# The boundary between two state-space batches and the head of the attention block, rearranged in a macaron block on one Trainium2 core

## The chip, the cores and the metric

The program runs on one NeuronCore of a Trainium2 chip. A core has a matrix engine (TensorE, PE in the profile), a vector engine (VectorE, DVE), a scalar engine (ScalarE, ACT), a general one (GpSimd, POOL) and a sync engine (SyncE, SP) that issues most of the DMA transfers. Each engine works through its own queue in order; engines meet at semaphores. The metric is the device time of one execution in microseconds. A profiled execution gives the time of every instruction, its "span" being the time from the first instruction to the last.

## What is computed

Two layers of a macaron network on x of 2 batches x 512 tokens x 256 features, each sublayer behind a layer norm:

```
x = x + 0.5 * ffn(norm(x))        # FFN0: silu(x W1) * (x W3), Hadamard transform, W2
x = x + state_space(norm(x))      # MAMBA
x = x + 0.5 * ffn(norm(x))        # FFN1
x = x + 0.5 * experts(norm(x))    # MOE0: 8 experts, top 2, and a shared one
x = x + attention(norm(x))        # ATTN: 16 heads, causal, ALiBi
x = x + 0.5 * experts(norm(x))    # MOE1
```

The state-space sublayer, cut to what matters (512 inner features, 16 states, 128 ranks):

```
xp, z = split(x @ W_in.T)
xc = silu(causal_conv4(xp) + conv_b)
dt, Bm, Cm = split(xc @ W_x.T)                 # 128, 16, 16 columns
delta = softplus(dt @ W_dt.T + b_dt)
h_t = exp(delta_t * A) * h_(t-1) + delta_t * B_t * xc_t     # over 512 tokens
y = (sum over states of h * C) + xc * Dp
out = (y * silu(z)) @ W_out.T
```

## The kernel before, in words

Every engine has its own program, written out by hand, and all waits are `wait_ge` on semaphores at constants. The stages run in the order FFN0(batch 0), MAMBA(0), MAMBA(1), FFN1(1), MOE0(0), MOE0(1), ATTN(0), MOE1(0), ATTN(1), MOE1(1); FFN0 of batch 1 and FFN1 of batch 0 are cut into "side pieces" that TensorE does inside the state-space loops. Features lie on partitions, 512 tokens along the free axis; the 512 inner features are four chunks c = 0 to 3 of 128.

**One state-space batch** (`mamba(b)` in each engine's program). Ahead of the loop, TensorE projects the four chunks of xc: `step_input(k)` adds chunk k to dt, `row_input(k)` adds chunk k to the 32 rows of B and C (three copies, 96 rows). For batch 1 these run in the last two steps of batch 0's loop and at the head of batch 1. ScalarE copies dt out of its bank (`dtT`), TensorE makes four delta products (`step_output(c)`), and ScalarE takes a softplus of each (`softplus(c)`, semaphore `delta`). The B rows are split into three bf16 parts by turns: ScalarE's `part(0..2)`, VectorE's `left(0..1)`. ScalarE's copy `c_rows` (semaphore `crows`) is what SP writes to DRAM and reads back broadcast over the partitions, one row of C a step. VectorE's (or for chunks 2 and 3 GpSimd's) `delta_input` makes dx = delta * xc.

**The loop** has 32 steps: half 0 (t = 0 to 15) does chunks 0 and 1 with state n = t, half 1 chunks 2 and 3. In step t:
- ScalarE: two exponentials `decay` (line 1534), three buffers deep, so it can be up to three steps ahead of the scans.
- TensorE: `broadcast_b(t+1)` (line 934) puts row n of B on all partitions of bank 0, after `mul` of step t; then `add_state(t-2)` (line 882) adds h * C into two banks of sums; then whatever else is placed in the step.
- VectorE: `times_b(t)` (line 2056), two products of dx with bank 0; `scan(t)` (line 2064), two scans.
- GpSimd: h * C (line 2391), three buffers deep.

In batch 1's loop there is more: TensorE opens batch 0's output banks with the residual (`open_state_output`), adds the four chunks of batch 0's output (`mamba_output(0, c)`, line 843, in the steps of `OUTPUT_AT`), opens the sums (`open_sums`, line 941, step 1) and projects the four gates of batch 1 (`mamba_gate(1, c)`, in the steps of `GATE_AT`; ScalarE copies them out raw in those of `GATE_OUT`, each ahead of its next step's exponentials). ScalarE takes batch 0's last sums out in step 1 (`sums_out(1, 0)`) and moves the residual out in step 7; VectorE's step 6 begins with the norm statistics of that residual. The banks of delta chunks 2 and 3 in batch 1 are 1 and 6, the same as batch 0's output banks.

**The late head** (`late_head`). In MOE0(1), TensorE goes through 13 blocks p: up products of chunk p, then point 0, then the broadcast of the expert weights and the down chunk p-2, then point 1. At these points it does the head of ATTN(0): two norm transposes (line 510), six projections of keys, queries and values, two value transposes (line 711), all through bank 7, each after the evacuation of the one before. ScalarE evacuates and casts, VectorE subtracts, SP writes the parts to DRAM and reads them back into the stacks of the score products.

Of the kernel before, what the change touches and what calls it, by code (L numbers as in the profile page):

```python
# [59 lines left out]
GATE_AT, GATE_OUT = (1, 4, 6, 8), (4, 7, 9, 11)  # L60
NORM_BANKS = ((7, 1), (1, 6))
OUTPUT_AT = (0, 1, 2, 3)
# [13 lines left out]
LATE_NORM_AT, LATE_HEAD_AT, EARLY_CAST_AT = 3, 5, 4  # L76
START_PRODUCTS, TAIL_PRODUCTS = 4, (8, 12)
EPS = 1e-5
HEAD = 4
# [74 lines left out]
def build(nc, x, W_in, conv_w, conv_b, W_x, W_dt, b_dt, A_log, Dp, W_out, W1, W2, W3, Wq, bq, Wk, bk,  # L154
          Wv, bv, Wo, bo, gate_w, w1, w2, w3, sw1, sw2, sw3, const_f, const_b, aux_q, aux_k, out):
    ctx = ExitStack()
    with ctx:
# [279 lines left out]
        class TensorProgram:  # L437
# [277 lines left out]
            def late_head(self, p, point):  # L715

                pe = self.pe
                if p == LATE_NORM_AT + 1:
                    pe.wait_ge(S[MOE0]["prod"], HEAD + MM + SECOND_MIXED + 1)
                    self.norm_transpose(2 * ATTN + 1, point)  # L720
                if LATE_HEAD_AT <= p < LATE_HEAD_AT + 3:
                    i = 2 * (p - LATE_HEAD_AT) + point
                    self.head_projection(0, i, LATE_BANKS[i], i)
                if p == LATE_HEAD_AT + 3:
                    self.head_values(0, point, 7, 6)
# [132 lines left out]
            def mamba(self, b):  # L858
# [60 lines left out]
                else:  # L919
                    step_input(3).then_inc(s["dt"], 1)  # L920
                    row_input(3).then_inc(s["bc"], 1)
# [31 lines left out]
                else:  # L953
                    add_state(STEPS - 1, 0)
                    pe.wait_ge(s["delta"], 2 * EC)
                for t in range(STEPS):
# [13 lines left out]
                    if b == 1:  # L970
                        if t in OUTPUT_AT:
                            if t == OUTPUT_AT[0]:
                                self.open_state_output(0)
                            self.mamba_output(0, OUTPUT_AT.index(t))
# [11 lines left out]
                    if b == 0 and t == STEPS - 2:  # L986
                        step_input(0, 1)
                        step_input(1, 1)
                    if b == 0 and t == STEPS - 1:
                        step_input(2, 1)  # L990
                        for k in range(EC - 1):
                            row_input(k, 1)
# [180 lines left out]
        class ScalarProgram:  # L1173
# [189 lines left out]
            def late_head(self, p):  # L1363

                if p == LATE_NORM_AT + 1:
                    self.norm_evacuate(2 * ATTN + 1, 0)
                first = LATE_HEAD_AT
                if first <= p < first + 3:
                    for i in (2 * (p - first), 2 * (p - first) + 1):
                        self.head_evacuate(0, i, LATE_BANKS[i])  # L1370
                if p == first + 3:
                    for c in range(DC):
                        self.head_values(0, c, 7)
# [86 lines left out]
            def mamba(self, b):  # L1460
# [28 lines left out]
                else:  # L1489
# [4 lines left out]
                    self.mamba_silu(1, 3)  # L1494
                act.wait_ge(s["dt"], b + 1)
# [1122 lines left out]
```

## Time and profile before

| | us |
|---|---|
| three timed runs | 796.66, 796.93, 798.0 |
| their median | 796.93 |
| the profiled execution's own time | 796.57 |
| its span | 794.8 |
| TensorE, VectorE, ScalarE, GpSimd busy in it | 708.7, 548.7, 405.4, 243.1 |

Times in the profile are counted from the start of its span. PE is TensorE's matmuls, PEld its weight loads, which overlap them. Matmul records overlap, so the time that a matmul takes of the engine is read from start to start. An fp32 matmul shows as two records. "idle before <-releaser" names what ended the engine's wait. "PEclk" is the clock granted to TensorE as a share of 2.4 GHz.

### The profile page before, as it was taken

The page shows a single profiled execution, that of the slowest core. Times are in us where ns is not written, and L with a number is a line of the kernel's source. Part 1 is how long each engine was busy: PE and PEld are TensorE (multiplying, and loading weights), DVE is VectorE, ACT ScalarE, POOL GpSimd, SP SyncE. Part 2 cuts the span into 40 slices and gives each one's busy share as a digit, 9 for nine tenths or more (in the row PEclk, how much of TensorE's full clock was granted, in tenths as well). Part 3 has the DMA queues.
Part 4 walks back from the last instruction along what each step waited for, and adds up shares of the span by engine and source line. Part 5 has one row for each costly group of instructions (what it writes and reads, how often), then busy time and mean ns, then how long its engine had stood idle before and what let it go on. Part 6 is the DMA issues. An engine that isn't in the chain of part 4 may idle for free.

```text
span 794.8 us, 10884 instructions
## 1 busy us (share of the span) xinstructions
PE 708.7 (89%) x4044; PEld 485.9 (61%) x4067; DVE 548.7 (69%) x962; ACT 405.4 (51%) x594; POOL 243.1 (31%) x190
## 2 busy tenths in 40 slices
PE   3899998796789699989999998997889999788998
PEld 3587664451325255547877887885447887434787
DVE  4544489999969999985448566367855656954644
ACT  3454597777447787751233344351476442274322
POOL 0001148777527677970799000001000001000000
PEclk9999999996899899999999999998999999899999
DMA  8300022223102222216100100043000033000000
GB/s 285 137 2 0 1 57 79 79 69 76 56 22 73 67 71 76 79 55 201 46 1 1 23 1 1 14 111 104 15 1 1 15 95 115 18 28 1 1 1 26
DMA packets 30609, 41.78 MB, mean 53 GB/s; under 512 B 3769, under 2 KB 19971, under 8 KB 30531
## 3 DMA queue, kind: packets, MB, share of 16 engines
q1 hardware_dynamic: 29306, 40.91, 16.9%
q8 instruction: 32, 0.52, 0.3%
q10 hardware_dynamic: 1252, 0.19, 0.2%
q14 instruction: 19, 0.16, 0.1%
HBM read 36.73 MB, written 4.26 MB: 52 GB/s over the span
## 4 chain that ended last, share of the span: by engine, by line
PE 54%; DVE 15%; issue 15%; ACT 7%; DMA 4%; POOL 2%; SPq 1%; another core or an unknown queue 0%; DVEq 0%; POOLq 0%; ACTq 0%
PE PS L500 32%; DVE PS L2056 4%; PE PS L605 3%; DVE shared L2064 3%; PE PS L1088 3%; PE PS L1071 2%; DVE route L2114 2%; POOL shared L2391 2%; DMA shared<-scratch_q 2%; PE PS L649 2%; ACT shared L1608 2%; PE PS L458 1%; PE PS L882 1%; DMA route<-scratch_c 1%; DMA shared<-in_L_ffn_W_dram 1%
## 5 line engine op out<-in xcount | busy, mean ns | idle before, releaser
L2391 POOL TENSOR_TENSOR shared<-shared,route 128x1024 f32<-128x1024 f32 x64 | 150.7, 2358 | 71.1 <-DVE shared L2064 71.1
L2064 DVE TENSOR_TENSOR_SCAN shared<-shared,PS 128x512 f32<-128x512 f32 x128 | 148.7, 1203 | 2.4 <-ACT shared L1534 1.7
L500 PE MATMUL PS<-xnT,work_r 128*128 128x512 f32 (+1 forms) x596 | 149.9, 398 | 0.3
L500 PE MATMUL PS<-xnT,weights_r 128*128 128x256 f32 (+1 forms) x732 | 148.6, 351 | 1.4 <-issue 1.1
L500 PEld LDWEIGHTS PS<-xnT,weights_r 128*128 128x128 f32 x732 | 114.4, 193 | 47.7 <-issue 33.4
L500 PEld LDWEIGHTS PS<-xnT,work_r 128*128 128x128 f32 (+1 forms) x596 | 109.2, 188 | 24.9 <-DVE gated L1788 1.6
L1534 ACT ACTIVATE shared<-shared,cols 128x512 f32<-128x512 f32 x128 | 85.0, 714 | 25.9 <-DVE shared L2064 25.4
L500 PE MATMUL PS<-weights_r,work_r 128*128 128x256 f32 (+1 forms) x624 | 88.6, 293 | 0.3 <-DVE work_r L1795 0.3
L2056 DVE TENSOR_TENSOR PS<-shared,PS 128x512 f32<-128x512 f32 x128 | 81.3, 681 | 3.4 <-PE PS L934 3.0
L500 PEld LDWEIGHTS PS<-weights_r,work_r 128*128 128x128 f32 (+1 forms) x624 | 80.4, 190 | 2.2 <-issue 0.6
L882 PE MATMUL PS<-shared,cf 64*64 64x512 f32 x512 | 75.9, 665 | 0.6 <-POOL shared L2391 0.6
L2477 POOL MEMSET shared<- 128x512 f32 x2 | 1.1, 526 | 222.8 <-DMA scratch_q<-shared 117.6
L1788 DVE TENSOR_TENSOR gated<-gated,PS 128x512 f32<-128x512 f32 (+1 forms) x48 | 32.8, 684 | 36.0 <-ACT gated L1253 35.9
L934 PE MATMUL PS<-combT,cb 96*128 96x512 bf16 x64 | 26.0, 407 | 34.1 <-DVE PS L2056 33.2
L1260 ACT ACTIVATE work_r<-gated 128x512 fp32r<-128x512 f32 (+1 forms) x48 | 30.3, 631 | 50.5 <-DVE gated L1913 41.2
L1253 ACT ACTIVATE gated<-PS 128x512 f32<-128x512 f32 (+1 forms) x48 | 28.5, 594 | 47.2 <-PE PS L500 47.0
L2114 DVE TENSOR_REDUCE route<-PS 128x2 f32<-128x256 f32 (+2 forms) x64 | 48.1, 819 | 2.2 <-PE PS L1052 1.2
L1795 DVE TENSOR_TENSOR work_r<-gated,work_r 128x512 fp32r<-128x512 f32 (+1 forms) x48 | 34.3, 716 | 20.8 <-ACT work_r L1260 20.2
L934 PEld LDWEIGHTS PS<-combT,cb 96*128 96x128 bf16 x64 | 6.3, 98 | 55.5 <-DVE PS L2056 50.6
L1913 DVE TENSOR_TENSOR gated<-gated,PS 128x512 f32<-128x512 f32 x40 | 27.4, 686 | 16.0 <-remote 14.6
L1803 DVE TENSOR_TENSOR shared<-gated,PS 128x512 f32<-128x512 f32 x16 | 10.9, 687 | 39.0 <-PE PS L605 34.7
L1608 ACT ACTIVATE shared<-PS 128x1280 f32<-128x1280 f32 x20 | 24.8, 1238 | 20.5 <-PE PS L1075 18.4
(224 smaller groups left out, 1049.9 us busy)
## 6 DMA issues: line engine op xcount, KB each, us to landing
route<-scratch_c SPq DMA_DIRECT2D x64, 256.0 KB, 3.2
shared<-in_L_ffn_W_dram SPq DMA_DIRECT2D x3, 1024.0 KB, 8.9
scratch_k<-shared SPq DMA_DIRECT2D x12, 128.0 KB
scratch_q<-shared SPq DMA_DIRECT2D x12, 128.0 KB
shared<-scratch_k SPq DMA_DIRECT2D x8, 192.0 KB
shared<-scratch_q SPq DMA_DIRECT2D x8, 192.0 KB
mamba_w<-in_L_ffn_w_dram SPq DMA_DIRECT2D x2, 704.0 KB, 5.3
beside<-in_L_ffn_w_dram SPq DMA_DIRECT2D x2, 704.0 KB, 7.8
```

Source lines behind the costliest of these rows:

```text
L500: last = nc.tensor.matmul(o, lhs[l], rhs[r], start=(start and i == 0), stop=(stop and i == 2))
L882: last = nc.tensor.matmul(bank(SUM_BANKS[j])[o, :], ident[r, r], hc[r, (t % H_SLOTS * 2 + j) * T:(t % H_SLOTS * 2 + j + 1) * T], start=Fal ...
L934: nc.tensor.matmul(bank(B_BANK), pick[0:96, n:n + 1].broadcast_to([96, P]), bc_stack[0:96, :], start=True, stop=True).then_inc(s["B"], 1)
L1260: nc.scalar.activation(ring[p % RING][0][0:rows, :], gated[0:rows, slot * T:(slot + 1) * T], ACT.Copy)\
L1534: nc.scalar.activation(decay[t % D_SLOTS][:, j * T:(j + 1) * T], delta_of[b][c], ACT.Exp, scale=c_A[:, n + c * DS:n + c * DS + 1]).then_in ...
L1608: nc.scalar.activation(pT[h % P_SLOTS], bank(score_bank(h), 3)[:, 0:PT_COLS], ACT.Exp)\
L1788: return nc.vector.tensor_tensor(g, g, bank(2 + slot if rows == P else slot)[0:rows, :], ALU.mult)
L1795: nc.vector.tensor_tensor(lo[0:rows, :], gated[0:rows, slot * T:(slot + 1) * T], hi[0:rows, :], ALU.subtract).then_inc(s["hid"], 1)
L2056: v.tensor_tensor(products[:, j * T:(j + 1) * T], dx[:, c * T:(c + 1) * T], bank(B_BANK), ALU.mult).then_inc(s["mul"], 1)
L2064: v.tensor_tensor_scan(hst[:, (t % 2 * 2 + j) * T:(t % 2 * 2 + j + 1) * T], decay[t % D_SLOTS][:, j * T:(j + 1) * T], products[:, j * T:(j ...
L2114: v.reduce_max(m_all.rearrange("p (h c) -> p h c", c=TC)[:, bass.ds(g * 2, 2), qc], tile, AX.X).then_inc(s["max"], 1)
L2391: nc.gpsimd.tensor_tensor(hc[:, u * 2 * T:(u * 2 + n) * T].rearrange("p (c t) -> p c t", c=n), hst[:, (t % 2) * 2 * T:(t % 2 * 2 + n) * T] ...
```

## The change

Five edits, each on the engines that it concerns:
1. Batch 1's row products: in step 30, two low-rank and two row products (before: two low-rank); in step 31 the other two of each (before: one low-rank, three row products; the last of each at the head of batch 1).
2. ScalarE loads the Softplus table ahead of the wait for dt, not behind the dt copy; a wait for batch 0's third-last state sum is added there; softplus(1) goes ahead of the C rows' copy.
3. In batch 1, softplus(2) and softplus(3) move into the loop behind step 2's exponentials, between a load of the Softplus table and one of the table with exp. The waits for them change: TensorE waits for two softplus ahead of the loop and for all four in step 2; VectorE no longer waits for the third ahead of step 0.
4. Batch 0's outputs go to steps 2, 2, 3, 3 (before 0, 1, 2, 3), the opening of their banks to step 2 (before 0); batch 1's gates to steps 3, 5, 6, 8 (before 1, 4, 6, 8), copied out in 6, 7, 9, 11 (before 4, 7, 9, 11).
5. The late head's pieces start at point 1 of block 4 and take one point each. Before, both transposes took block 4, the projections blocks 5 to 7, the value transposes block 8.

```diff
-GATE_AT, GATE_OUT = (1, 4, 6, 8), (4, 7, 9, 11)
+GATE_AT, GATE_OUT = (3, 5, 6, 8), (6, 7, 9, 11)
-OUTPUT_AT = (0, 1, 2, 3)
+OUTPUT_AT, LATE_DELTA = (2, 2, 3, 3), 2
-LATE_NORM_AT, LATE_HEAD_AT, EARLY_CAST_AT = 3, 5, 4
+LATE_NORM_AT, LATE_SLOT, LATE_HEAD_AT, EARLY_CAST_AT = 3, 9, 5, 4
...
             def late_head(self, p, point):        # TensorE
                 pe = self.pe
-                if p == LATE_NORM_AT + 1:
+                i = 2 * p + point - LATE_SLOT
+                if i == 0:
                     pe.wait_ge(S[MOE0]["prod"], HEAD + MM + SECOND_MIXED + 1)
-                    self.norm_transpose(2 * ATTN + 1, point)
-                if LATE_HEAD_AT <= p < LATE_HEAD_AT + 3:
-                    i = 2 * (p - LATE_HEAD_AT) + point
-                    self.head_projection(0, i, LATE_BANKS[i], i)
-                if p == LATE_HEAD_AT + 3:
-                    self.head_values(0, point, 7, 6)
+                if 0 <= i < DC:
+                    self.norm_transpose(2 * ATTN + 1, i)
+                if DC <= i < DC + 6:
+                    self.head_projection(0, i - DC, LATE_BANKS[i - DC], i - DC)
+                if DC + 6 <= i < 2 * DC + 6:
+                    self.head_values(0, i - DC - 6, 7, 6)
...
                 else:                             # TensorE, batch 1
-                    step_input(3).then_inc(s["dt"], 1)
-                    row_input(3).then_inc(s["bc"], 1)
                     pe.wait_ge(s["dtT"], 2)
...
                     add_state(STEPS - 1, 0)
-                    pe.wait_ge(s["delta"], 2 * EC)
+                    pe.wait_ge(s["delta"], EC + 2)
...
-                        if t in OUTPUT_AT:
-                            if t == OUTPUT_AT[0]:
-                                self.open_state_output(0)
-                            self.mamba_output(0, OUTPUT_AT.index(t))
+                        if t == OUTPUT_AT[0]:
+                            pe.wait_ge(s["delta"], 2 * EC)
+                            self.open_state_output(0)
+                        for c in range(EC):
+                            if OUTPUT_AT[c] == t:
+                                self.mamba_output(0, c)
...
                     if b == 0 and t == STEPS - 2:
                         step_input(0, 1)
                         step_input(1, 1)
+                        row_input(0, 1)
+                        row_input(1, 1)
                     if b == 0 and t == STEPS - 1:
                         step_input(2, 1)
-                        for k in range(EC - 1):
-                            row_input(k, 1)
+                        row_input(2, 1)
+                        step_input(3, 1).then_inc(s["dt"], 1)
+                        row_input(3, 1).then_inc(s["bc"], 1)
...
             def late_head(self, p):               # ScalarE
-                if p == LATE_NORM_AT + 1:
-                    self.norm_evacuate(2 * ATTN + 1, 0)
                 first = LATE_HEAD_AT
-                if first <= p < first + 3:
-                    for i in (2 * (p - first), 2 * (p - first) + 1):
-                        self.head_evacuate(0, i, LATE_BANKS[i])
-                if p == first + 3:
-                    for c in range(DC):
-                        self.head_values(0, c, 7)
+                for i in (2 * p - LATE_SLOT, 2 * p + 1 - LATE_SLOT):
+                    if 0 <= i < DC:
+                        self.norm_evacuate(2 * ATTN + 1, 0, (i,))
+                    if DC <= i < DC + 6:
+                        self.head_evacuate(0, i - DC, LATE_BANKS[i - DC])
+                    if DC + 6 <= i < 2 * DC + 6:
+                        self.head_values(0, i - DC - 6, 7)
...
+                nc.scalar.preload_act_table(ACT.Softplus)          # ScalarE, mamba(b)
                 act.wait_ge(s["dt"], b + 1)
+                act.wait_ge(s["ys"], HEAD + b * (STEPS - 2))
                 nc.scalar.activation(dtT, bank(DT_BANK[b]), ACT.Copy).then_inc(s["dtT"], 1)
-                nc.scalar.preload_act_table(ACT.Softplus)
...
                 part(1, 64, bc_rest)
+                softplus(1)
                 nc.scalar.activation(c_rows, bank(BC_BANK[b])[0:2 * DS, :], ACT.Copy).then_inc(s["crows"], 1)
-                softplus(1)
                 act.wait_ge(s["left"], 2 * b + 2)
                 part(2, 32, bc_rest)
-                softplus(2)
-                softplus(3)
+                if b == 0:
+                    softplus(2)
+                    softplus(3)
...
+                    if b == 1 and t == LATE_DELTA:
+                        nc.scalar.preload_act_table(ACT.Softplus)
+                        softplus(2)
+                        softplus(3)
+                        nc.scalar.preload_act_table_set("natural_log_exp_and_others")
...
                 first_input(1)                    # VectorE, mamba(b)
-                dve.wait_ge(s["delta"], b * EC + 3)
+                if b == 0:
+                    dve.wait_ge(s["delta"], 3)
```

## Rows read from the trace of the kernel before

**Rows 1.** The page: busy time of each engine, and the chain of waits by engine.
```profile
PE 708.7 (89%) x4044; PEld 485.9 (61%) x4067; DVE 548.7 (69%) x962; ACT 405.4 (51%) x594; POOL 243.1 (31%) x190
...
PE 54%; DVE 15%; issue 15%; ACT 7%; DMA 4%; POOL 2%; SPq 1%; another core or an unknown queue 0%; DVEq 0%; POOLq 0%; ACTq 0%
```

**Rows 2.** Windows: us; busy time (instructions) of PE, PEld, DVE, ACT, POOL; clock; DMA.
```profile
237.80:354.30 116.50, 102.12 (x595) 56.51 (x591) 114.50 (x145) 86.56 (x124) 89.08 (x45) 0.96 0.24 73
...
470.90:542.00 71.10, 68.42 (x378) 56.86 (x382) 38.90 (x85) 34.36 (x57) 0.53 (x1) 1.00 0.16 43
```

**Rows 3.** Waits of VectorE, both state-space batches: us in total, times, longest.
```profile
DVE shared L2033 <- ACT combT L1510: 5.3, 1, 5.3
```

**Rows 4.** Timeline of VectorE, head of batch 1: start, us, what [idle before].
```profile
237.81 1.29 DVE L2056 TENSOR_TENSOR PS<-shared,PS 128x512 f32<-128x512 f32 x2 [1.38 <-PE PS L934]
239.49 2.33 DVE L2064 TENSOR_TENSOR_SCAN shared<-shared,PS 128x512 f32<-128x512 f32 x2 [0.38 <-ACT shared L1534]
...
246.67 2.33 DVE L2064 TENSOR_TENSOR_SCAN shared<-shared,PS 128x512 f32<-128x512 f32 x2 [0.24 <-POOL shared L2391]
...
252.33 1.27 DVE L2056 TENSOR_TENSOR PS<-shared,PS 128x512 f32<-128x512 f32 x2
...
255.75 1.27 DVE L2056 TENSOR_TENSOR PS<-shared,PS 128x512 f32<-128x512 f32 x2
```

**Rows 5.** Windows, the end of batch 0's loop.
```profile
222.40:231.30 8.90, 8.90 (x28) 3.21 (x24) 5.54 (x7) 1.22 (x2) 4.70 (x2) 0.91 0.00 0
```

**Rows 6.** Timeline of ScalarE at the boundary.
```profile
230.71 0.60 ACT L1496 ACTIVATE shared<-PS 128x512 f32<-128x512 f32 x1 [5.47 <-PE PS L864]
231.33 1.28 ACT L1497 ACT_TABLE_LOAD   x1
232.62 0.59 ACT L1510 ACTIVATE combT<-PS 96x512 bf16<-96x512 f32 x1
...
234.57 0.57 ACT L1517 ACTIVATE shared<-PS 32x512 f32<-32x512 f32 x1
...
236.14 1.23 ACT L1506 ACTIVATE shared<-PS,cols 128x512 f32<-128x512 f32 x2
...
238.68 2.56 ACT L1534 ACTIVATE shared<-shared,cols 128x512 f32<-128x512 f32 x4
```

**Rows 7.** Timeline of TensorE at the boundary.
```profile
235.28 1.10 PE L889 MATMUL PS<-shared 128*128 128x512 f32 x2 [1.08 <-ACT shared L1517]
...
237.33 0.39 PE L934 MATMUL PS<-combT,cb 96*128 96x512 bf16 x1
```

**Rows 8.** Timeline of TensorE, steps 1 and 2 of batch 1.
```profile
243.29 1.88 PE L941 MATMUL PS<-shared,skips 128*128 128x512 f32 x4
245.01 1.89 PE L843 MATMUL PS<-shared 128*128 128x256 f32 x8
...
248.12 0.39 PE L934 MATMUL PS<-combT,cb 96*128 96x512 bf16 x1
248.44 1.09 PE L882 MATMUL PS<-shared,cf 64*64 64x512 f32 x8
249.46 1.99 PE L843 MATMUL PS<-shared 128*128 128x256 f32 x8
```

**Rows 9.** Windows, steps 5 to 8 of batch 1 (granted clock behind POOL).
```profile
258.70:261.56 2.86, 0.00 (x0) 0.00 (x0) 2.78 (x12) 2.20 (x3) 2.86 (x2) 1.00 0.26 92
261.60:268.40 6.80, 5.22 (x16) 2.27 (x16) 6.80 (x11) 4.42 (x8) 2.60 (x2) 0.50 0.12 41
```

**Rows 10.** Timeline of TensorE, block 4 of MOE0(1).
```profile
490.76 0.63 PE L510 MATMUL PS<-cf,xn_tok 128*128 128x128 f32 x4 [1.69 <-issue]
...
493.76 0.63 PE L510 MATMUL PS<-cf,xn_tok 128*128 128x128 f32 x4 [0.74 <-DVE xnT L1771]
```

**Rows 11.** Timeline of VectorE in the same block.
```profile
489.27 1.38 DVE L1759 TENSOR_SCALAR xn_tok<-x_tok,stats 128x256 f32<-128x256 f32 x4
...
492.93 0.68 DVE L1771 TENSOR_TENSOR xnT<-PS,xnT 128x512 fp32r<-128x512 f32 x1
```

## The prediction, made before the changed kernel was run

> **What bounds the kernel now.** I read the page first: TensorE is busy 89% of the span and leads the chain of waits, with VectorE second [rows 1]. A share over the span says little about one boundary, so next came the windows by stage. In the second state-space batch (237.80 to 354.30) VectorE is busy 114.50 of 116.50 us, TensorE 102.12; in the second batch of the first expert stage (470.90 to 542.00) TensorE is busy 68.42 of 71.10 us, VectorE 38.90 [rows 2]. So the two places that the diff touches have different limits: there a microsecond counts if VectorE gets it, here if TensorE does. The table of VectorE's waits over both state-space batches is led by one single wait of 5.3 us, for ScalarE's first part copy at the head of the second batch [rows 3]: that is the boundary. The timelines of the boundary, engine by engine, give the sizes.
>
> VectorE's clock in the loop is one step: two products with B (line 2056), two scans (line 2064), 3.42 us from 252.33 to 255.75. Step 0 of the second batch starts at 237.81, step 5 at 255.75; I call these starts T0 and T5 [rows 4]. The loop has one hard coupling: broadcast_b(t+1) stands at the head of TensorE's step t and its one bank is free only when step t's products are done. Whatever TensorE does after broadcast_b(t+1) must be over before broadcast_b(t+2), or step t+2 starts late.
>
> **Row products in the last two steps: nothing.** Eight products and one add_state lie between 222.4 and 231.3, and TensorE is busy 8.90 of these 8.90 us [rows 5]. The change reorders them; the dt row is still the last but one, so ScalarE's copy of dt stays at about 230.71. The two low-rank row products now wait for the third silu, done before 225. The new wait on ys asks for an add_state that precedes dt in the same queue: nothing.
>
> **ScalarE across the boundary: a gain of 0.4 at T0, 1.3 by T2.** The Softplus table load (1.28 us at 231.33, after the dt copy) moves into the idle 5.47 us before that copy [rows 6]. The first part copy then starts when the bc row is ready, about 231.57 instead of 232.62. From there I follow the chain with the old durations and hand-overs: softplus(0) 232.53, the first remainder 232.27 to 232.95, part 1 at 233.1, softplus(1) 233.64, the C rows, now behind softplus(1), 234.21 to 234.78 (before, 234.57 to 235.14), part 2 ends at 235.3. TensorE's step_output(3) waits for the C rows: 0.36 earlier than 235.28. Add_state and broadcast_b(0) follow 2.05 later, so T0 moves from 237.81 to 237.45 [rows 4, 6, 7]. Two softplus (1.23 us) leave the path ahead of the exponentials: these start near 236.6 instead of 238.68, which removes the scan's 0.38 us wait; the sums, the GpSimd gate products behind them and GpSimd's step 0 come 2 us earlier, which removes a 0.24 us wait at step 2 [rows 6]. T1 = 240.87 and T2 = 244.29; step 2's scan comes near 245.4 instead of 246.67, 1.3 earlier.
>
> The same swap at the first batch is worth nothing: there the bc row comes later than the load, and step 0 waits for work that stays in place.
>
> **The two late softplus inside the loop: nothing.** ScalarE ends the sums at 241.0, step 2 at 242.2, then a load, two softplus (done at 244.75), a load (245.95), step 3's exponentials to 247.2. The scan that needs them starts near 248.9, and TensorE's new wait is reached after 246.9. If that cover were gone, the cost would be the 3.8 us of the insert.
> The Trainium skill (ScalarE: Activation LUTs, What ACT_TABLE_LOAD costs) adds a drain of about 1.4 us to every switch. In this trace the copy follows its load without it (231.33 + 1.28, next at 232.62). By the page the insert would end 2.8 us later, at the edge of that scan.
>
> **Four output products in two steps instead of four: the loss.** TensorE's matmuls overlap in the records, so I count from start to start [rows 8]: broadcast 0.32, add_state 1.02, a two-bank opening 1.72 (243.29 to 245.01), the next output and gate group together 3.11 (245.01 to 248.12), of which I give the output 1.71 and the gate 1.40; before a broadcast 0.1 more. The old order had open + output in step 0, opening + output + gate in step 1 (4.8), one output each in 2 and 3. The new one is empty in step 0, 2.0 in step 1, and then:
> step 2: 0.32 + 1.02 + 1.72 + 2 x 1.71 + 0.1 = 6.6 us;
> step 3: 0.32 + 1.02 + 2 x 1.71 + 1.40 + 0.1 = 6.3 us.
> VectorE takes 3.42 for each. Broadcast_b(3) can't go before step 2's products are through, T2 + 1.32 = 245.6. So broadcast_b(5) goes at 245.6 + 12.9 = 258.5, and T5, 0.45 later, is 258.9. Old T5: 255.75. That is **+3.2 us** with all of it at full clock, the 1.3 of gain already inside. What waits behind: every later broadcast, add_state and side product on TensorE, hence VectorE's steps 4 and 5. After step 3 only one gate lies in a step, so nothing more is lost, and nothing is won back: VectorE is the limit for the remaining 26 steps. ScalarE stands at raw gate 0 until about 259, then delivers the residual about 1 us before VectorE's statistics want it.
>
> **The clock: 0 to 1.5 us more.** The granted clock was 1.00 while TensorE idled from 258.70 to 261.56, and then 0.50 (1.2 instead of 2.4 GHz) from 261.60 to 268.40 [rows 9]. The new steps 0 and 1 leave TensorE idle from about 239.3 to 242.2. If the low level falls on the opening, broadcast and add_state behind that gap, these 3 us of work take up to twice as long, of which up to 1.5 us reaches T5. I laid low stretches of half and of all the length of that row over the new steps at ten positions, each beginning within 4 us after 240: they give 0.1 to 1.65 more, mean 0.8. I take 0.9.
> The Trainium skill (TensorE: Matmul & The Clock Gate, HAM oscillation — how this bites in real kernels) says that waits between bursts make the next burst start cold; the trace agrees (0.50 after 2.9 us of nothing). It speaks against bunching these products.
>
> **The late head half a block on: -2.4 us.** In block 4 TensorE finished the up products at 489.07, stood 1.69 us before the first norm transpose, did it, the broadcast and the down chunk in 2.26 (493.76 less 0.74 less 490.76), and stood 0.74 before the second transpose [rows 10]. The transposes wait for VectorE's scaled rows (489.27 + 1.38 = 490.65) and low halves (492.93 + 0.68 = 493.61) [rows 11]. Half a block on, broadcast and down chunk (2.26 less 0.4 for the transpose) fill the first wait, the transpose follows at about 490.9, the next up products, some 2.9 us, fill the second, until 494. Both waits go: 2.43. The second transpose at 494, ScalarE's evacuation and VectorE's low half put the first projection's input at about 496.1, and TensorE is there at about 496: 0.1 back. Projections and value transposes are the same count at the same price; their evacuations and casts come about 2.5 us earlier too, so the writes and stack loads on SP's queue shift with them. The bounds: 0 if each wait reappears, 2.5 if none does. I take 2.4, since TensorE has no other wait until 542.
>
> **Sum against the profiled execution** (796.57 us, span 794.8): +3.2 + 0.9 - 2.4 = +1.7. The median of the runs is 796.93, 0.36 above the profiled one, so 798.6. This kernel's runs can tell about 0.2%, 1.6 us, from no change; the forecast stands on that edge.
>
> **Rivals.**
> 1. Forecast: overfull steps with a partly slow clock, both head waits gone. +1.2 to +2.4, 798.1 to 799.3. Chance 0.45.
> 2. The same, but the clock stays at 2.4 GHz: +3.2 - 2.4 = +0.8, 797.7. For it: the low stretch may fall into the gap itself. Against: gaps of 2.9 us did lower it. 0.20.
> 3. The head's waits only move: the first projection waits for ScalarE's late evacuation in block 5. +3.2 + 0.7 = +3.9, 800.8. Against: the order worked out above leaves 0.1. 0.12.
> 4. More waits in steps 5 to 9: ScalarE, held at raw gate 0, is late with the residual, so VectorE's statistics wait, or a low clock falls on the side products: +1 on the forecast, 799.6. The margin is about 1 us. 0.11.
> 5. Faster: VectorE keeps its 1.3 and the bunched outputs are absorbed, -1.3 - 2.4 = -3.7, 793.2. This needs steps 2 and 3 on TensorE at no more than about 4 us each; above that T5 slips. Against: 3.11 us for one output and one gate. For: the old step 1 took 4.8 and VectorE didn't stop. 0.06.
> 6. The parts cancel or are hidden elsewhere, 796.9. 0.06.
>
> **From these:** slower by over 0.2%: 0.25 of case 1, 3 and 4, together 0.48; within: 0.20 of case 1, 2 and 6, together 0.46; faster: 0.06. Range 796.8 to 800.8: cases 1, 2, 4, 6 and half of 3.
>
> **What would show it.** T0 near 237.45, T2 near 244.3; then VectorE waiting twice for the broadcast, about 2.5 and 2.5 us, T5 at 259 to 260.4; a clock of 0.50 somewhere in 240 to 248; exponentials without waits; in block 4 of the expert stage no wait before either transpose. I am wrong if VectorE's steps 3 to 5 stay 3.42 apart, or if TensorE waits anew at the first projection.

## The result, and the profile after

The changed kernel is slower. Over 11 runs of each the median went from 797.03 to 801.18 us, 4.15 apart (the means are 3.5 apart). The ratio on record is 1.0038 with a 95% interval of 1.0024 to 1.0052, which is 1.9 to 4.1 us, 3.0 in the middle; the text goes by this ratio. I had forecast +1.7 (798.6), a range of 796.8 to 800.8, and a chance of 0.48 for slower. From the forecast's base of 796.93 the ratio leads to 800.0, inside the range; the median of the 11 runs lies 0.4 above its top. The profiled execution, 802.7 us with a span of 800.9, is the slowest of its 11 runs, while that of before, 796.57, lies a little under its median. So the 6.1 us between the two traces are more than the 3.0 between the kernels, and part of the work below was to find which of the 6.1 belong to the change.

I followed VectorE's instructions through both traces, each against the same instruction of before, and noted by how much it starts later:

| place | before | after | shift |
|---|---|---|---|
| T0, step 0 of batch 1 | 237.81 | 236.91 | -0.9 |
| T4 | 252.33 | 253.34 | +1.0 |
| T5 | 255.75 | 259.62 | +3.9 |
| step 20 | 311.98 | 318.41 | +6.4 |
| MOE0(0), up to its fifth block | 411 to 440 | | +6.1 to +8.2 |
| MOE0(1), ahead of the late head | 487 | | +8.6 |
| MOE0(1), behind it | 529.34 | | +6.0 |
| end of the span | | | +6.1 |

The view that shows the first step is VectorE's timeline after [rows 4]; each line is start, duration, what, and in brackets the wait ahead of it.

```profile
236.91 1.29 DVE L2067 TENSOR_TENSOR PS<-shared,PS 128x512 f32<-128x512 f32 x2 [2.26 <-PE PS L933]
...
253.34 1.29 DVE L2067 TENSOR_TENSOR PS<-shared,PS 128x512 f32<-128x512 f32 x2 [2.65 <-PE PS L933]
...
259.62 1.29 DVE L2067 TENSOR_TENSOR PS<-shared,PS 128x512 f32<-128x512 f32 x2 [2.76 <-PE PS L933]
```

The two waits of 2.65 and 2.76 us for broadcast_b (line 933 now) are the two that the forecast put there at about 2.5. TensorE's timeline says why [rows 8]:

```profile
238.35 0.38 PE L933 MATMUL PS<-combT,cb 96*128 96x512 bf16 x1 [0.46 <-DVE PS L2067]
241.68 0.61 PE L933 MATMUL PS<-combT,cb 96*128 96x512 bf16 x1 [2.95 <-DVE PS L2067]
242.08 3.62 PE L940 MATMUL PS<-shared,skips 128*128 128x512 f32 x4
245.49 0.63 PE L933 MATMUL PS<-combT,cb 96*128 96x512 bf16 x1
246.06 1.66 PE L883 MATMUL PS<-shared,cf 64*64 64x512 f32 x8
247.64 1.98 PE L856 MATMUL PS<-x_tok,cf 128*128 128x512 f32 x4
249.47 3.62 PE L844 MATMUL PS<-shared 128*128 128x256 f32 x16
252.92 0.38 PE L933 MATMUL PS<-combT,cb 96*128 96x512 bf16 x1
253.23 1.09 PE L883 MATMUL PS<-shared,cf 64*64 64x512 f32 x8
254.25 3.72 PE L844 MATMUL PS<-shared 128*128 128x256 f32 x16
257.62 1.74 PE L500 MATMUL PS<-xnT,weights_r 128*128 128x512 f32 x6
259.20 0.39 PE L933 MATMUL PS<-combT,cb 96*128 96x512 bf16 x1
```

From broadcast to broadcast, step 2 takes 7.43 us (245.49 to 252.92) and step 3 6.28 (252.92 to 259.20). Forecast were 6.6 and 6.3 at full clock. The difference in step 2 is the clock: the broadcast at 245.49 takes 0.63 instead of 0.38, add_state 1.66 instead of 1.09. It was low from the gap in step 1 on [rows 9]; windows of us, busy time (instructions) of PE, PEld, DVE, ACT, POOL, granted clock, DMA:

```profile
238.95:242.00 3.05, 0.32 (x1) 0.33 (x2) 3.05 (x5) 2.97 (x6) 2.76 (x3) 0.74 0.07 28
242.00:247.30 5.30, 5.30 (x14) 1.45 (x13) 5.30 (x7) 5.26 (x7) 4.34 (x2) 0.50 0.22 49
```

ScalarE did what it should: the loads and the two softplus of step 2 are done at 245.6, and its wait at raw gate 0 ends at 259.39 [rows 6].

```profile
241.76 1.28 ACT L1565 ACT_TABLE_LOAD   x1
243.05 1.26 ACT L1510 ACTIVATE shared<-PS,cols 128x512 f32<-128x512 f32 x2
244.33 1.28 ACT L1568 ACT_TABLE_LOAD   x1
245.63 3.78 ACT L1539 ACTIVATE shared<-shared,cols 128x512 f32<-128x512 f32 x6
...
259.39 0.60 ACT L1506 ACTIVATE shared<-PS 128x512 f32<-128x512 f32 x1 [7.95 <-PE PS L500]
...
261.11 1.07 ACT L1574 ACTIVATE x_tok<-PS 128x512 f32<-128x512 f32 x2
```

The residual is out at 262.2 and VectorE's statistics begin at 263.08 without a wait. The late head has lost both waits [rows 10]; TensorE's timeline, in which a down chunk (12 records of 256 columns), the first transpose (line 510), the up products (512 columns) and the second transpose follow one another:

```profile
497.56 1.78 PE L500 MATMUL PS<-weights_r,work_r 128*128 128x256 f32 x12
499.31 0.63 PE L510 MATMUL PS<-cf,xn_tok 128*128 128x128 f32 x4
499.70 3.03 PE L500 MATMUL PS<-xnT,work_r 128*128 128x512 f32 x12
502.56 0.60 PE L510 MATMUL PS<-cf,xn_tok 128*128 128x128 f32 x4
```

What I had not forecast is the jump at step 20. Long behind the change, TensorE opens the sums of the second half (line 940) in its step 18, behind broadcast_b(19), and that opening waits for ScalarE to empty the banks. First the trace of before, TensorE and VectorE:

```profile
307.09 1.98 PE L941 MATMUL PS<-shared,skips 128*128 128x512 f32 x4 [1.18 <-ACT shared L1542]
...
311.55 0.39 PE L934 MATMUL PS<-combT,cb 96*128 96x512 bf16 x1
```

```profile
311.98 1.29 DVE L2056 TENSOR_TENSOR PS<-shared,PS 128x512 f32<-128x512 f32 x2 [0.86 <-PE PS L934]
```

Then the changed kernel, in the same order:

```profile
309.59 0.39 PE L933 MATMUL PS<-combT,cb 96*128 96x512 bf16 x1
311.88 3.59 PE L940 MATMUL PS<-shared,skips 128*128 128x512 f32 x4 [1.90 <-ACT shared L1547]
...
316.45 1.69 PE L500 MATMUL PS<-xnT,weights_r 128*128 128x256 f32 x12
317.98 0.39 PE L933 MATMUL PS<-combT,cb 96*128 96x512 bf16 x1
```

```profile
318.41 1.29 DVE L2067 TENSOR_TENSOR PS<-shared,PS 128x512 f32<-128x512 f32 x2 [3.23 <-PE PS L933]
```

The opening took 3.59 us and not 1.98, the side products (line 500) follow it, and broadcast_b(20) comes at 317.98; VectorE's step 20 waits 3.23 us for it. In the trace of before the same wait was 0.86 us, with an opening of 1.98 us behind a wait of 1.18.

### The profile page after: what moved, and what is told of

It reads as the page before. It is cut to its first block, busy times and chain, and to the rows that moved or that the text cites. A ratio compares the mean times of both kernels' runs of the same rounds, so it can differ in the third digit from the quotient of the medians.

```text
span 800.9 us, 10910 instructions
## 1 busy us (share of the span) xinstructions
PE 714.7 (89%) x4067; PEld 488.7 (61%) x4067; DVE 550.7 (69%) x962; ACT 408.0 (51%) x596; POOL 242.2 (30%) x190
## 4 chain that ended last, share of the span: by engine, by line
PE 65%; DVE 14%; issue 10%; ACT 7%; DMA 2%; POOL 1%; SPq 0%; DVEq 0%; POOLq 0%; ACTq 0%
PE PS L500 36%; DVE PS L2067 4%; PE PS L605 3%; PE PS L883 3%; DVE route L2125 3%; PE PS L1092 3%; PE PS L1075 2%; DVE shared L2075 2%; PE PS L649 2%; PE PS L844 2%; PE PS L865 2%; ACT shared L1618 2%; ACT shared L1539 1%; PE PS L767 1%; PE PS L458 1%
## 5 line engine op out<-in xcount | busy, mean ns | idle before, releaser
L1805 DVE TENSOR_TENSOR work_r<-gated,work_r 128x512 fp32r<-128x512 f32 (+1 forms) x48 | 36.5, 761 | 18.5 <-ACT work_r L1264 18.0
```

The costliest lines, as they stand in the source:

```text
L1805: nc.vector.tensor_tensor(lo[0:rows, :], gated[0:rows, slot * T:(slot + 1) * T], hi[0:rows, :], ALU.subtract).then_inc(s["hid"], 1)
```

## The experiments

All ratios are to the kernel before, timed on the same chip. "Shift" is again VectorE's, in the profiled execution, against the trace of before.

**The parts, one by one.** Five kernels, each with some of the five edits of the diff:

```diff
 e1: before + edit 5 (late head)
 e2: after - edit 5
 e3: before + edit 1 (row products) + edit 2 (table load, softplus(1))
 e4: before + edits 1, 2 and 5
 e5: before + edit 4:
-GATE_AT, GATE_OUT = (1, 4, 6, 8), (4, 7, 9, 11)
+GATE_AT, GATE_OUT = (3, 5, 6, 8), (6, 7, 9, 11)
-OUTPUT_AT = (0, 1, 2, 3)
+OUTPUT_AT = (2, 2, 3, 3)
```

> The kernel before with the late head alone half a block on. Theory A (each edit is worth what its own place shows, the head takes two waits of 1.69 and 0.74 us off TensorE in block 4): 2.4 us faster than before, no wait before either norm transpose, nothing changed up to 489. Theory B (the head's waits only move and the rest of the fall between 497 and 503 in the changed kernel is something else): within 0.5 us of before.

Measured: 0.9986, interval 0.9964 to 1.0009. The shift goes from +1.09 at 487 to -1.41 at 529: **-2.50 us across the head**. The same difference stands in every one of the ten traces with edit 5, -2.47 to -2.51, and it is 0.0 in those of e2, e3 and e5. The ratio alone could not have said so; the trace does.

> The changed kernel with the late head put back. Theory A: slower than before by the boundary alone, +4 at step 5 and with what a low clock adds behind it +4 to +7, so 2.4 slower than the changed kernel. Theory B: the same as the changed kernel, +3 to +4. If the wait at step 20 belongs to the boundary, it is here too.

Measured: 1.0054, interval 1.0029 to 1.0080. T0 -1.4, T5 +3.5, step 20 +6.15, and +6.3 from 487 to 536 without the head's gain. So the change's loss is in the state-space part, and the late head gives back part of it. The trace ends at +8.7: 1.8 of that comes between 536 and 600, most of it at the collision told of further down, which this execution had.

> The kernel before with the row products in the last two steps, the Softplus table ahead of the dt copy and softplus(1) ahead of the C rows; all four softplus, the outputs and the gates where they were. Theory A: step 0 starts 0.5 to 0.9 earlier, the scan's 0.38 wait goes, and the kernel is 0.8 to 1.3 us faster. Theory B (VectorE's earlier start is given back to TensorE at steps 1 to 3, which carries 4.8 us in step 1, or at the wait of step 19 or 20): within 0.4 us of before.

Measured: 0.9996, interval 0.9974 to 1.0017. T0 -0.9, and -0.9 to -1.2 from there to the attention block. What VectorE has at T0 is carried, but it is too small for the ratio, which excludes neither theory; and the last part shows that only 0.4 of it comes from the edits.

> The two together, without the late softplus and the bunched outputs. Theory A: the sum of the two, 3.2 to 3.7 us faster than before, about 793.5. Theory B: one of the two is given back, 1 to 2.4 us faster.

Measured: 0.9954, interval 0.9936 to 0.9972: faster than both kernels, as theory A had it. T0 -1.4, behind the head -4.0.

> The kernel before with the outputs in steps 2, 2, 3, 3, their banks opened in step 2 and the gates in steps 3, 5, 6, 8 (out in 6, 7, 9, 11), nothing else. Theory A (the bunched products are the whole loss): steps 0 to 3 start where they did, VectorE waits for the broadcast at steps 4 and 5, step 5 starts 3.7 to 4.7 later than before, and with the wait at step 20 the kernel is 4 to 6.5 us slower. Theory B (the loss comes from the two softplus and their table loads in ScalarE's step 2, or from both together): less than 2 us slower.

Measured: 1.0085, interval 1.0054 to 1.0115 over 7 runs. T0 +0.05, T4 +1.2, **T5 +4.1**, flat from there on to 354. The profiled execution was one of the two fastest of the seven (800.57 of 799.36 to 806.72), so its trace has less in it than the ratio, and no jump at step 20. The ratio is +4.3 to +9.2 us, which fits theory A and not B. The bunched outputs alone make the loss at T5; without edits 1 to 3 it is no smaller. Between T0 and T5 the clock was low only from 242.7 to 246.1 here, ahead of step 2's broadcast, and the two overfull steps take 6.61 us (246.53 to 253.14) and 6.29 (253.14 to 259.43).

**The clock in the gap.** In e6 TensorE does bf16 products into an idle bank in the empty steps 0 and 1; nobody reads them.

```diff
+                        if t < 2:
+                            self.idle_products(7, (10, 6)[t])
                         if t == OUTPUT_AT[0]:
```

> The changed kernel with products that nobody reads on TensorE in steps 0 and 1 of batch 1 (ten and six, 128x512 bf16, into the free bank 7, behind the broadcast of each step). They fill the idle stretch of 3 us ahead of the opening of the sums. Theory A: the granted clock stays at 1.00 between 237 and 248, the opening takes 1.7 instead of 3.4 us, step 5 starts about 1 us earlier (+2.9 instead of +3.9), and the kernel is 1 us faster than the changed one, more if the later low stretches go too. Theory B (the low stretch costs nothing there, since the two bunched steps wait for VectorE anyway): step 5 at the same time within 0.2.

Measured: 1.0023, interval 1.0003 to 1.0044. TensorE's timeline and two windows of e6:

```profile
239.25 2.32 PE L517 MATMUL PS<-cb 128*128 128x512 bf16 x10
...
242.59 1.88 PE L940 MATMUL PS<-shared,skips 128*128 128x512 f32 x4
...
245.78 0.39 PE L933 MATMUL PS<-combT,cb 96*128 96x512 bf16 x1
...
252.39 0.38 PE L933 MATMUL PS<-combT,cb 96*128 96x512 bf16 x1
...
258.68 0.39 PE L933 MATMUL PS<-combT,cb 96*128 96x512 bf16 x1
```

```profile
238.90:247.30 8.40, 7.46 (x32) 2.88 (x33) 8.40 (x10) 8.28 (x12) 7.12 (x4) 1.00 0.18 63
307.00:315.00 8.00, 6.42 (x38) 3.87 (x37) 7.60 (x9) 7.32 (x11) 6.01 (x4) 1.00 0.27 76
```

With the gap filled the clock stays at 2.4 GHz, the opening takes 1.88 us instead of 3.62, and the two overfull steps take 6.61 us (245.78 to 252.39) and 6.29 (252.39 to 258.68): the forecast's 6.6 and 6.3. From T0 to T5 VectorE needs 21.52 us, against 22.71 after and 17.94 before. So of the 4.8 us that the change adds between T0 and T5, 3.6 are the count of products in two steps and 1.2 the low clock. T5 itself came at +3.4 and not at the +2.9 expected, as T0 lay 0.7 later than in the trace of the change; and the ratios of e6 and the change overlap, so the 1.2 rests on the traces. At step 18 the clock is full too, and the shift does not grow there.

**Another spread of the same work.** The outputs over steps 2, 3, 4, 4, and the first gate pushed on to step 5.

```diff
-GATE_AT, GATE_OUT = (3, 5, 6, 8), (6, 7, 9, 11)
+GATE_AT, GATE_OUT = (5, 6, 7, 8), (6, 7, 9, 11)
-OUTPUT_AT, LATE_DELTA = (2, 2, 3, 3), 2
+OUTPUT_AT, LATE_DELTA = (2, 3, 4, 4), 2
```

> The changed kernel with outputs in steps 2, 3, 4, 4 and gates in 5, 6, 7, 8 (out in 6, 7, 9, 11); the two softplus stay in step 2. Theory A: TensorE's steps take 4.8, 3.1, 4.8, 2.9 us, VectorE's step 5 starts where it would without any wait (about 254.0, 5.6 earlier than in the changed kernel); the residual is then late for VectorE's statistics in step 6 by 1 to 2 us; in all 3.5 to 4.5 us faster than the changed kernel. Theory B (the inserted table loads are what holds the loop): no faster than the changed kernel by more than 1 us.

Measured: 1.0170, interval 1.0142 to 1.0198, by far the slowest: my expectation failed. T5 was at 256.66, only 0.9 late, as I had wanted, but then ScalarE and VectorE (timelines of e7):

```profile
263.88 0.60 ACT L1506 ACTIVATE shared<-PS 128x512 f32<-128x512 f32 x1 [10.74 <-PE PS L500]
...
265.60 1.07 ACT L1574 ACTIVATE x_tok<-PS 128x512 f32<-128x512 f32 x2
```

```profile
266.71 0.42 DVE L1722 BATCH_NORM_STATS2 stats<-x_tok 128x6 f32<-128x256 f32 x1 [6.55 <-issue]
...
279.13 0.18 DVE L1758 RECIPROCAL stats<-stats 128x4 f32<-128x4 f32 x1 [6.61 <-ACT stats L1229]
```

ScalarE stands at raw gate 0 for 10.74 us, because the gate is now one of TensorE's last products before it. The residual's copy is behind that gate in ScalarE's queue, and VectorE's step 6 begins with the statistics of that residual: 6.55 us of waiting, where I had expected 1 to 2. This is the mechanism of the forecast's rival 4. In the change itself it has a margin of 0.9 us (262.2 to 263.08); here it is overdrawn. The same happens once more: ScalarE waits 9.10 us for raw gate 1, the square root of the statistics (line 1229) stands behind it, and VectorE's reciprocal at 279.13 waits 6.61 us for that, with TensorE's clock at 0.50 from 265.8 to 276.0. These two waits are most of what VectorE loses from T5 (+0.9) to step 14 (+16.4), and the jump at step 20 adds 2.1.

**The queue at step 18.** In e8, which is the whole change otherwise, the side products of step 18 go ahead of the opening, where they fill TensorE's wait for ScalarE.

```diff
+                    if b == 1 and t == DS + 2:
+                        for n in pieces_at(b, t):
+                            self.side_piece(b, n)
                     if t == DS + 2:
                         pe.wait_ge(s["yr"], b * 4 + 2)
...
-                    for n in pieces_at(b, t):
+                    for n in pieces_at(b, t) if (b, t) != (1, DS + 2) else ():
```

> The changed kernel with the side products of batch 1's step 18 ahead of the opening of the second sums instead of behind it. Theory A (the second loss, 2.4 us at step 20, is a queue on TensorE: it stands idle for ScalarE's copies of the sums with work behind it, falls to the low clock and opens the sums at half speed): the idle 1.9 us shrinks below 0.6, the opening takes 1.7, step 20's wait of 3.2 goes, 2 to 3 us faster than the changed kernel. Theory B (VectorE waits for something else there): no difference beyond 0.5 us.

Measured: 0.9999, interval 0.9981 to 1.0017, where the change has 1.0038 and, in the repeat below, 1.0032. T5 +4.1, step 20 +3.5: the loss at step 20 is gone, and of the wait of 0.86 us that was there before, 0.11 is left. The interval lies clear of the change's first one and overlaps that of its repeat a little. TensorE's timeline of e8:

```profile
309.79 0.39 PE L933 MATMUL PS<-combT,cb 96*128 96x512 bf16 x1
309.83 1.77 PE L500 MATMUL PS<-xnT,weights_r 128*128 128x256 f32 x12
312.13 1.98 PE L940 MATMUL PS<-shared,skips 128*128 128x512 f32 x4 [0.52 <-ACT shared L1550]
...
315.06 0.39 PE L933 MATMUL PS<-combT,cb 96*128 96x512 bf16 x1
```

**The gains together, and two repeats.** e9 is e4 with the edit of step 18; e10 is e4 once more; e11 is the change once more. The expectation of e9 names the last two softplus inside the loop among its parts; the kernel that ran does not have them there (it has edits 1, 2 and 5, as e4).

> The kernel before with the edits to the row products, to ScalarE's order (the table load ahead of the dt copy, softplus(1) ahead of the C rows, the last two softplus inside the loop) and the late head, the outputs left at steps 0 to 3, and with batch 1's side products of step 18 placed ahead of the opening of the second half's sums. My theory: the parts add. The ScalarE and head edits alone gave 0.9954; in the kernel before, VectorE waited 0.86 us at step 20 for the broadcast behind the opening, and this wait goes, so about 0.9 us more: ratio 0.994 to the kernel before, VectorE's shift constant from step 5 to step 31. Rival: the opening no longer has a wait to fill, the side products only change places and the broadcast of step 20 is as late as before: ratio 0.9954 and the shift constant too, but the wait of 0.86 us still there.

> The kernel with the edits to the row products, ScalarE's order and the late head alone, once more, on the same chip as the kernel with the step 18 placement added, so that the two can be compared. Expected: ratio 0.9954 to the kernel before again, within 0.9936 to 0.9972; if the step 18 placement is worth 0.9 us, the other one lies 0.001 below this one; if it is worth nothing, they agree.

> The whole change once more, beside the others on one chip. My theory says +3.9 at step 5 (bunched outputs with a partly low clock), about +2.4 at step 20 where the opening of the second sums holds the broadcast while TensorE's clock is low, some +1.8 in the expert stage between, and -2.5 at the late head; ratio about 1.004. Rival to the part at step 20: it is a chance of that one execution. Then this profile shows no growth of VectorE's shift between steps 12 and 31, and the runs scatter over 3 us with or without it.

Measured: e9 0.9946, 0.9926 to 0.9966, median 793.17 and its 6 runs from 792.62 to 794.52. e10 0.9977, 0.9954 to 1.0000, median 795.65 and its 12 runs from 791.05 to 800.52. e11 1.0032, 1.0010 to 1.0054, 10 runs from 796.91 to 803.75. e10's ratio lies just above the 0.9936 to 0.9972 that I expected from e4, the same kernel. Their intervals overlap, and what the traces give to that kernel's edits, 0.4 us at the boundary and 2.5 at the head, is 0.9964, between the two. Two things follow from the traces. e11's has +5.05 from T0 to T5 (238.22 to 261.21) and +2.5 at step 20, so the loss at step 20 isn't a chance of one execution; of the +1.8 expected in the expert stage it has +0.8. And e10's trace, of a kernel **without** bunched outputs, shows the jump at step 20 too: the shift goes from -0.9 to +1.5 there, where in e4 it stays at -1.4. So the jump isn't the change's own. Windows of e10, then of e4, at the same two places:

```profile
276.60:283.40 6.80, 6.49 (x26) 3.50 (x30) 6.52 (x9) 3.01 (x5) 3.49 (x3) 0.51 0.25 58
307.20:310.60 3.40, 3.40 (x8) 0.87 (x11) 3.03 (x4) 3.38 (x5) 2.04 (x1) 0.50 0.29 97
```

```profile
277.70:281.10 3.40, 3.40 (x20) 2.61 (x12) 3.40 (x5) 1.44 (x2) 2.07 (x1) 0.50 0.23 77
304.50:309.40 4.90, 3.73 (x19) 1.68 (x19) 4.90 (x6) 4.84 (x7) 3.31 (x2) 1.00 0.16 58
```

In e10 the low stretch of steps 10 to 12 lasts 6.8 us, TensorE and ScalarE come out of it some 0.7 us further behind VectorE, the opening of step 18 waits 1.92 us instead of 1.17, and the clock falls as it begins: 3.58 us instead of 1.98. Of the eleven traces whose side products stand behind the opening and whose schedule is otherwise that of before from step 9 on, five (after, e2, e7, e10, e11) had the long stretch, a longer wait of 1.6 to 1.9 us and the slow opening, and six (before, e1, e3, e4, e5, e6) a low stretch of 3.4 us, 1.2 us of waiting and the fast one. What makes the stretch long or short stays open. With the side products ahead, the long stretch came as well in e8 and e9, 6.8 us, and cost nothing: the wait is 0.5 or 0.3 us and the opening takes 1.98. VectorE has no wait at step 20 in e9's trace, so the rival in that expectation is out. e9's six runs lie within 1.9 us, but e8's twelve, with the same edit, scatter over 5.0 (794.80 to 799.75), so it isn't shown that the edit narrows the runs; nor can its 0.86 us be told from the ratios of e9 and e10, whose intervals overlap.

**A collision that e9's trace showed.** At 536 the profiled execution of e9 lost 1.7 us to something new. VectorE and GpSimd, timelines of e9:

```profile
536.48 2.73 DVE L1954 TENSOR_TENSOR work_r<-gated,work_r 128x256 fp32r<-128x256 f32 x2 [0.27 <-ACT work_r L1286]
```

```profile
536.23 2.37 POOL L2488 TENSOR_TENSOR x_tok<-x_tok,bo_all 128x1024 f32<-128x1024 f32 x1
```

Two subtractions that take 0.76 us elsewhere took 2.73, and TensorE waited 1.50 us for them. GpSimd's add stands behind a wait for writes to DRAM, and starts between 536 and 558 us in these traces. In e12 it waits for VectorE:

```diff
                 pool.wait_ge(xn_done, 2 * ATTN + b + 1)
+                if b == 0:
+                    pool.wait_ge(S[MOE0]["hid"], HEAD + 2 * MM)
```

> The kernel before with the edits to the row products, to ScalarE's order ahead of the loop and to the late head, with batch 1's side products of step 18 ahead of the opening, and with one wait more: GpSimd adds the attention's output bias to batch 0's tokens only after VectorE's last low halves of the second expert batch. In the profile without that wait the add of 2.37 us began 0.25 us ahead of VectorE's two subtractions of 256 columns, these took 2.73 us instead of 0.76, and TensorE's last down products waited 1.50 us for them. My theory: the two engines share the way to SBUF in such operations, so with the wait the subtractions take 0.76 us again in every execution, TensorE has no wait there, and the executions in which the two met get 1.7 us faster: median 792.5 to 793.2 against about 797.3 for the kernel before, ratio 0.9935 to 0.9945. Rival: the slow subtractions had another cause, such as a DMA into the same tiles: then they are seen at 2.7 us again in some executions. Second rival: the later add now meets VectorE's residual or its attention work and costs the same there: no gain, and an operation of VectorE behind 537 longer than before.

Measured: 0.9948, interval 0.9928 to 0.9968, median 792.72 and 6 runs from 791.47 to 794.01. Timelines of VectorE and GpSimd in e12:

```profile
535.49 0.76 DVE L1954 TENSOR_TENSOR work_r<-gated,work_r 128x256 fp32r<-128x256 f32 x2 [0.28 <-ACT work_r L1286]
...
537.91 1.29 DVE L1784 SCALAR_TENSOR_TENSOR x_tok<-PS,x_tok 128x512 f32<-128x512 f32 x2 [1.67 <-PE PS L500]
```

```profile
537.94 2.35 POOL L2490 TENSOR_TENSOR x_tok<-x_tok,bo_all 128x1024 f32<-128x1024 f32 x1
```

The subtractions take 0.76 us, and the residual beside the add takes 1.29 as ever (one of its inputs is in PSUM). The ratio is that of e9, and just above the 0.9935 to 0.9945 expected: the collision was rare, in 2 of the 13 other traces (e2 and e9), so the median can't show it, and one trace of e12 isn't proof that it can't come back.

## Why the forecast came out as it did

The mechanism was right and its sizes nearly so; a loss further on was missing.

- **Row products, ScalarE across the boundary.** Forecast T0 237.45, measured 236.91 [rows 4, 6]. From the start of the dt copy to T0 it was 7.10 us before and 6.68 after, so 0.42 of gain where I had 0.36. This is the edits' own: it is 7.10 in all three traces without edits 1 and 2 (before, e1, e5) and 6.68 to 6.74 in the eleven with them. The rest is that the dt row itself came 0.48 us earlier, and that is scatter as far as can be told: in those eleven the copy starts between 229.7 and 231.9 (before: 230.71), and T0 scatters from -1.4 to +0.8. T2 was at 243.77 (forecast 244.29), and the waits of the scan and of step 2's scan are gone.
- **The late softplus: nothing.** Right as far as the traces show; no run has this edit alone. Done at 244.31 with the second load at 245.6, and nobody waits. The activations behind the two loads start 1.29 and 1.30 us after the loads do (241.76 to 243.05, 244.33 to 245.63). The drain of about 1.4 us that the Trainium skill (ScalarE: Activation LUTs, What ACT_TABLE_LOAD costs) adds to every switch is at neither.
- **Four outputs in two steps: +3.2.** Right. Steps of 6.61 and 6.29 us with the clock up (e6, and e5 too), 6.6 and 6.3 forecast.
- **The clock: +0.9.** Step 2 took 7.43 instead of 6.6. Forecast T5 was 258.9 + 0.9 = 259.8, measured 259.62; e6 against the change gives 1.2 us between T0 and T5, so the term was a little small. That T5 fits to 0.2 us is partly luck: from T0 to T5 it took 22.71 us where 22.35 was forecast (259.8 less 237.45), and T0 happened to lie 0.54 early. In e11, with T0 at 238.22, T5 was 261.21.
- **The late head: -2.4.** Measured -2.47 to -2.51 in ten traces. Neither rival 3's wait at the first projection nor another one appeared. (Rival 3's own sum leaves open where its 0.7 comes from; with the forecast's terms and nothing gained at the head it is +3.2 + 0.9 = +4.1.)
- **The step that failed: "After step 3 only one gate lies in a step, so nothing more is lost".** It holds to step 12 (+4.1) and fails at step 20. There the broadcast stands behind an opening that waits for ScalarE, and which the clock can double. I had looked for more waits in steps 5 to 9 (rival 4, 0.11) and had passed over the 0.86 us wait at step 20 in the trace of before, a place where TensorE was the late one already. The 2.4 us there come in some executions of either order; three of three traces of the change with its full loop (after, e2, e11) had them, and two of the eight others (e7, e10), which include e5 and e6 with their bunched outputs. That the change makes the jump more frequent fits these counts, and is not shown.
- **Between the traces only.** In MOE0(0) the profiled execution of the change lost 2.15 us more (411 to 440), with the clock at 0.50 from 431.6 to 435.0. But 0.9 of these were lost ahead of 431.6, in VectorE's small operations of the router, one of which, a cast of 128x32, took 0.77 us where it had taken 0.18 in the trace of before. The other traces drift by 0.0 to +0.8 there, so I take this as its own scatter.

The sum for the profiled pair: +3.9 at T5, +0.15 to step 12, +2.4 at step 20, -0.35 to 411, +2.15 and +0.3 in the expert stages, -2.5 at the head, +0.1 behind: +6.15. For the medians the last but the head are scatter, so by this pair the change is worth +1.4 in executions without the jump and +3.8 with it. That still counts the dt row's 0.48 us as a gain of the change. With T5 taken against the start of the dt copy, the four traces with the whole loop and no filler give +4.4 to +4.6 at T5 (after, e2, e8, e11), so about +2.0 without the jump, where the forecast had +1.7, and +4.4 with it. The measured +3.0 lies between either way. The runs of the change fall in two groups, 798.7 to 799.2 (4) and 800.7 to 802.7 (7), their means 2.6 apart; that the jump parts them fits, but only profiled executions can tell, and of the 11 that is one.

## What to carry to other kernels

Count, for an in-order engine with one coupling to the bottleneck in each step, the sum of its work between two couplings: what exceeds the bottleneck's step is lost for good, and the empty steps that pay for it are worse than useless if the clock falls in them. Search the trace for places where the engine that isn't the limit is late already, however little; a wait of 0.86 us in the trace of before became 3.2 us under a later low clock, and work that doesn't depend on the wait belongs ahead of it. When one part of a change loses and two gain, try the gains alone: they are at 0.9954 (e4) and 0.9977 (e10) of before, and at 0.9948 with the two further edits of e12, the whole change at 1.0038.

## What the runs showed of the hardware

- The low stretch of TensorE's clock in steps 10 to 12 was 3.4 us long in seven traces and 6.8 in the other seven, and it was 3.4 in e4 and 6.8 in e10, two executions of one kernel: its length isn't fixed by the program. In the five traces with the long one and the side products behind the opening, TensorE stood for 1.6 to 1.9 us, not 1.2, ahead of that opening some 30 us later, and the clock fell to 0.50 again, for 3.4 us. An fp32 opening of two banks took 1.9 to 2.0 us with the clock up and 3.5 to 3.7 with it low.
- VectorE's subtraction with both inputs in SBUF stood still while GpSimd's add ran: 2.73 and 2.61 us in the two traces in which the add had started first, 0.76 in the others. In e5 it was the other way round: the add started 0.07 us into VectorE's second subtraction, which took its usual 0.42 us, and the add took 2.61 instead of some 2.37. VectorE's residual with one input in PSUM took 1.29 us beside the same add. The Trainium skill (SBUF — State Buffer, Who interferes with whom) says just this: a `tensor_tensor` with two SBUF inputs and a GpSimd operation that reads SBUF exclude each other, and the one that starts second waits; both halves agree here.
